# Rotary embedding of queries and keys: the swap of neighbouring partitions by VectorE or by transfers inside SBUF

## The chip, the cores and the metric

One core of a Trainium2 chip runs the whole kernel. The metric is the device time of one execution in microseconds; the kernel before takes 3115.08 us, the median of three runs (3113.67 to 3115.29).

## The reference

Two layers of a transformer decoder over 8 sequences of 256 tokens with 512 features. Layer 0 is causal attention in a window of 64 tokens with rotary embedding, cross attention to a context, and a mixture of 64 experts; layer 1 is a state-space mixer, cross attention and a feed-forward part with low-rank experts. What matters here is the rotary embedding:

```python
def _rotate_half(t):
    x1 = t[..., ::2]
    x2 = t[..., 1::2]
    return jnp.stack((-x2, x1), axis=-1).reshape(t.shape)
...
qkv = x @ w_qkv.T
...
q = q * cos + _rotate_half(q) * sin
k = k * cos + _rotate_half(k) * sin
scores = jnp.einsum('bhqd,bhkd->bhqk', q, k) * scale
```

Features 2j and 2j+1 are exchanged, one with its sign turned, multiplied by a sine and added to the cosine product.

## The kernel before

Everything that the change touches is in phase 1 (`phase1`), the first 750 us of the span: local attention and cross attention, one sequence after the other, i = 0 to 7. The engines run five programs of their own (`block.sync`, `block.gpsimd`, `block.scalar`, `block.tensor`, `block.vector`), each in the order written, and meet through semaphores that count up; `due(name, i, k)` is the count for the k-th event of sequence i.

Queries and keys are made with features on partitions and tokens in the free dimension: eight chunks of 128 features (four of queries, four of keys), 256 tokens each. The exchanged features are therefore neighbouring partitions. For each chunk c:

- TensorE (`queries_keys`, line 757) makes the product in bank 2 + c % 2, from weights and columns split in a high and a low part, twelve products per chunk (line 730). From chunk 2 on it waits until the copy of the chunk two before has left the bank (line 761).
- ScalarE (lines 661 to 664) copies the bank to `qk_raw`, a view of the first 2048 columns of the tile `arena`. In sequence 0 it also makes the high part of a piece of weights after each copy (`split_hi`).
- For each pair of chunks, n = 0 to 3, GpSimd (line 563) multiplies by the cosines into one of two buffers, `cosq` and `rec`. The third product waits for the first rotation to be added (line 562), the fourth for the second. Between the second and the third GpSimd computes the rstd of the previous sequence's output (line 567).
- VectorE (`rope`, line 955) exchanges neighbouring partitions with a shuffle into `sinq` (line 959), multiplies by the sines (line 960), and adds the cosine product into `qk` (line 962).

VectorE's order around this, for i of 1 and more, is: the end of the previous sequence's cross attention (`delta`, `centred`), rotation 0, the additions of that delta with their statistics (`add_delta`, two halves, lines 987 to 989), rotations 1 to 3, then the minima of the scores (line 1058). In sequence 0 two pieces of weights are split in their low part (`split_lo`, line 1013) after each rotation: the key weights after rotations 0 and 1, the value weights after 2 and 3; TensorE waits for these before chunks 4 to 7 and before the values.

TensorE makes the first half of the values after the eight chunks (`values(i, 0)`, from the buffer `w_slot`), then the scores of the first pair of heads, which need the third rotation (line 776); the fourth is needed from the fifth pair on. The second half of the values follows the second pair's scores.

SyncE's queue brings the value weights back from HBM in four pieces of 512 KB, one after each of the first four chunks (lines 501 to 503), for every sequence but the first. Later in a sequence it moves the values by half a tile into `v_mid` with two transfers inside SBUF, 64 partitions of 2 KB each (lines 460 and 461). ScalarE issues no transfer in this phase; in phase 2 it issues those that store expert outputs (`expert_out`).

`arena` is used in turn by `qk_raw`, by the transposed probabilities of local attention (first 1536 columns) and, whole, by the probabilities of cross attention. Once, at the start, the window mask is loaded into its columns 2048 to 2303 and copied to bf16.

Of the kernel before, what the change touches and what calls it, by code (L numbers as in the profile page):

```python
# [28 lines left out]
ALU = mybir.AluOpType  # L29
# [8 lines left out]
P = 128  # L38
NSEQ, S, D = 8, 256, 512
T = NSEQ * S  # L40
NT = S // P
KC = D // P
# [3 lines left out]
HD = D // HEADS  # L46
# [32 lines left out]
probs_ready probsT_psum probsT_ready pv_psum lrec_ready lrecT_psum lrec_copied xk_psum xk_ready xv_psum  # L79
xv_ready xq_psum xq_ready xs_psum clipped_ready xprobs_ready xpv_psum xrec_ready xrecT_psum xrec_copied  # L80
xattn_ready delta_psum delta_taken clip_bounds rs_ready shared_in init1 x_in ctx_in mask_in rows_out
wq_in w_hi w_lo vs_in slot_a slot_b colsT_lo hrT0_hi
""".split()
TURN_SEMS_2 = """
hThi_ready hTlo_ready sd_hi sd_lo router_psum negmax_router exp_router gate_psum tanh_ready
# [6 lines left out]
dtabs_ready dtexp_ready dtone_ready dtln_ready dA_ready tri_ready bc_psum decay_psum decay_ready  # L92
w_ready xrows_psum xrows_ready xdt_ready y_psum gated_ready sumsq_ready gated_norm
s_psum smin_ready sexp_ready sT_psum sT_act sT_dve ret_psum x_out_ready yk_used
routes_in cx_in cxT_in yk0_in0
""".split()


# [102 lines left out]
def due(name, i, k):  # L201

    return i * PER_SEQ[name] + k
# [130 lines left out]
def phase1(nc, sy, const, dr, held, nseq=NSEQ):  # L334
# [6 lines left out]
    with ExitStack() as ctx:  # L341
        def sb(name, shape, dt=F32):
            return ctx.enter_context(nc.sbuf_tensor(name, shape, dt))
# [3 lines left out]
        cosT, sinT = sb("cosT", [P, S]), sb("sinT", [P, S])  # L347
# [11 lines left out]
        oT = sb("oT", [P, KC, S])  # L359
        arena = sb("arena", [P, 4096])  # L360
        qk_raw = arena[:, 0:2 * KC * S].rearrange("p (c s) -> p c s", c=2 * KC)
        wmask = arena[:, 2048:2048 + S]
        qk = sb("qk", [P, 2 * KC, S])
        xkT = sb("xkT", [P, KC, S])
        cosq, sinq = sb("cosq", [P, 2, S]), sb("sinq", [P, 2, S])
        swap = [p ^ 1 for p in range(HD)]
        v, v_mid, xv = sb("v", [P, NT, D]), sb("v_mid", [P, D]), held["xv"]
        probs = sb("probs", [P, 3, 2, S])
        probsT = arena[:, 0:3 * 2 * S].rearrange("p (b k s) -> p b k s", b=3, k=2)
        smin, ssum = sb("lmin", [P, LPAIRS, 2, 2]), sb("lsums", [P, KC, NT, HPC])  # L370
        xprobs = arena[:].rearrange("p (b t k s) -> p b t k s", b=4, t=NT, k=2)
# [221 lines left out]
        def _(act):  # L593
            def split_hi(u, n):
                if u >= V:
                    act.wait_ge(sy[f"slot_{'ab'[u % 2]}"], stored(u - 2))
                    act.wait_ge(sy["qk_proj"], due("qk_proj", 0, KC * (u - 1)))
                if u == XQ:
                    act.wait_ge(sy["w1b_in"], n_late * 16)
                else:  # L600
                    act.wait_ge(sy["wq_in" if u == Q else "w1_in"], 16 if u == Q else n_early * 16)
                act.activation(w_slot[u % 2][:, n, 0, :], raw_piece(u, n), ACT.Copy).then_inc(sy["w_hi"], 1)

            def cols_copy(at):
                for j in range(NT):
                    act.wait_ge(sy["rowsT_psum"], at + j + 1)
                    act.activation(hT2[0][:, :, j * P:(j + 1) * P],  # L607
                                   turned_bank(at, j)[:, :].rearrange("p (c t) -> p c t", c=KC), ACT.Copy
                                   ).then_inc(sy["colsT_ready"], 1)

            def keys_copy(i, first, end):

                for c in range(first, end):
                    act.wait_ge(sy["xk_psum"], due("xk_psum", i, c + 1))
                    act.activation(xkT[:, c, :], key_bank(i, c)[:, 0:S], ACT.Identity, bias=bk[:, c:c + 1]
                                   ).then_inc(sy["xk_ready"], 1)

            def values_copy(i, j):
                act.wait_ge(sy["v_psum"], due("v_psum", i, j + 1))
                act.activation(v[:, j, :], bank(6 + j)[:, :], ACT.Copy).then_inc(sy["v_ready"], 1)  # L620

            def copy_recips(i, c):
                act.wait_ge(sy["lrecT_psum"], due("lrecT_psum", i, c + 1))
                if c >= 2:
                    act.wait_ge(sy["attn_ready"], due("attn_ready", i, c - 1))
                act.activation(rec[:, c % 2, :], bank(4 + c % 2)[:, S:2 * S], ACT.Copy
                               ).then_inc(sy["lrec_copied"], 1)
# [32 lines left out]
            for i in range(nseq):  # L660
                for c in range(2 * KC):
                    act.wait_ge(sy["qk_proj"], due("qk_proj", i, c + 1))
                    act.activation(qk_raw[:, c, :], bank(2 + c % 2)[:, 0:S], ACT.Copy,
                                   scale=-QK_SCALE if c < KC else 1.0).then_inc(sy["qk_raw_ready"], 1)
                    if i == 0:
                        split_hi(K if c < KC else V, c % KC)
                values_copy(i, 0)
                for n in range(LPAIRS):
                    c, r = n // 2, 2 * (n % 2)
                    act.wait_ge(sy["lmin_ready"], due("lmin_ready", i, n + 1))  # L670
                    if n >= 3:
                        act.wait_ge(sy["probsT_psum"], due("probsT_psum", i, n - 2))
                    for k in range(2):
                        scores = bank_pair(2 * (n % 2))[:, k, :]
                        act.activation(probs[:, n % 3, k, 0:P], scores[:, 0:P], ACT.Exp, bias=smin[:, n, k, 0:1],
                                       scale=-1.0, accum_out=ssum[:, c, 0, r + k:r + k + 1])
                        act.activation(probs[:, n % 3, k, P:S], scores[:, P:S], ACT.Exp,
                                       bias=smin[:, n, k, 1:2], scale=-1.0,
                                       accum_out=ssum[:, c, 1, r + k:r + k + 1]).then_inc(sy["probs_ready"], 1)
                    if n == 1:  # L680
                        values_copy(i, 1)
                    if i == 0 and 2 <= n < 2 + KC:
                        split_hi(XQ, n - 2)
                    if n in (5, 7):
                        copy_recips(i, (n - 5) // 2)
                copy_recips(i, 2)
                copy_recips(i, 3)
                if i == 0:
                    act.wait_ge(sy["w1b_in"], n_late * 16)
                    keys_copy(0, 0, KC)  # L690
                cols_copy(turned_attn(i))
                for c in range(KC):
                    act.wait_ge(sy["xq_psum"], due("xq_psum", i, c + 1))
                    act.activation(qk[:, c, :], bank(6 + c % 2)[:, 0:S], ACT.Identity, bias=bq[:, c:c + 1]
                                   ).then_inc(sy["xq_ready"], 1)
                for n in range(LPAIRS):
                    act.wait_ge(sy["clipped_ready"], due("clipped_ready", i, 2 * n + 2))
                    act.activation(xprobs[:, n % 4], xprobs[:, n % 4], ACT.Exp, scale=1.0 / ROOT_HD
                                   ).then_inc(sy["xprobs_ready"], 1)
                    if i < last and n in (0, LPAIRS - 1):  # L700
                        keys_copy(i + 1, n // (LPAIRS - 1), n // (LPAIRS - 1) + 1)
                    if i == last:
                        shared_opening(n)
                if i < last:
                    cols_copy(turned_in(i + 1))
                    keys_copy(i + 1, 2, 3)
                else:
                    shared_chunks_hi(2, 4)
                for half in range(2):
                    act.wait_ge(sy["xrecT_psum"], due("xrecT_psum", i, half + 1))  # L710
                    act.activation((cosq, sinq)[half][:].rearrange("p c s -> p (c s)"), bank(half)[:, :], ACT.Copy
                                   ).then_inc(sy["xrec_copied"], 1)
                if i < last:
                    keys_copy(i + 1, 3, KC)
                else:
                    shared_chunks_hi(4, len(MS_CHUNKS))
# [234 lines left out]
        def _(dve):  # L951
            def ln(ins):
                sy.link(dve, "dve_link", ins)

            def rope(i, n):
                dve.wait_ge(sy["qk_raw_ready"], due("qk_raw_ready", i, 2 * n + 2))
                if n:
                    dve.wait_ge(sy["rope_ready"], due("rope_ready", i, n))
                ln(dve.stream_shuffle(sinq[:], qk_raw[:, 2 * n:2 * n + 2, :], swap))
                ln(dve.tensor_tensor(sinq[:], sinq[:], sinT[:].unsqueeze(1).broadcast_to([P, 2, S]), ALU.mult))  # L960
                dve.wait_ge(sy["rope_cos_ready"], due("rope_cos_ready", i, n + 1))
                dve.tensor_tensor(qk[:, 2 * n:2 * n + 2, :], cosq2[n % 2][:], sinq[:], ALU.add
                                  ).then_inc(sy["rope_ready"], 1)
# [74 lines left out]
            for i in range(nseq):  # L1038
# [13 lines left out]
                for n in range(LPAIRS + 2):  # L1052
# [7 lines left out]
                    if n >= 2:  # L1060
                        m = n - 2
# [2441 lines left out]
```

## Time and profile before

| | us |
|---|---|
| median of three runs | 3115.08 |
| the profiled execution | 3110.33 |
| its span | 3108.5 |
| TensorE products busy | 2954.8 |
| VectorE busy | 2301.0 |
| ScalarE busy | 1579.0 |
| GpSimd busy | 808.7 |

Phase 1 ends near 750 us. A sequence takes about 90 us, and its rotation lies in the first 16 of them. Shares of busy time over the span say which engine is full on average; what one step is worth is read from the timeline around it and from the waits that end there. A row of a timeline has the start, the duration, the engine, the line, the operation, output and inputs, shapes and count of the merged instructions, and in brackets the idle time before them with what ended it. All times are microseconds from the start of the span unless marked as nanoseconds.

### The profile page before, as it was taken

Reading aid. Unit: us, or ns where it says so; the run is one execution under the profiler, and the core shown is the slowest. Engines: PE = TensorE matmul, PEld = TensorE weight load, DVE = VectorE, ACT = ScalarE, POOL = GpSimd, SP = SyncE. Lnnn points to the kernel's source line nnn. Section 1 sums busy time; section 2 is a strip of 40 time slices with the busy share of each in tenths; the row PEclk is TensorE's granted clock in tenths of the full one; section 3 lists DMA queues with packets and bytes.
Section 4 is the critical chain, followed back from the end, with each engine's and each line's share of the span. In section 5 each row is a group of like instructions: output and inputs, shape, how many; then the busy total and the mean of one; then the engine's idle time right before and its main releaser. Section 6 shows DMA issues by size and latency. Waiting matters only on the chain. (4 is left out here: it accounts for less than half of the span.)

```text
span 3108.5 us, 61772 instructions
## 1 busy us (share of the span) xinstructions
PE 2954.8 (95%) x23073; PEld 2384.2 (77%) x23073; DVE 2301.0 (74%) x4321; ACT 1579.0 (51%) x3643; POOL 808.7 (26%) x974
## 2 busy tenths in 40 slices
PE   7999999998999999999999969999999989999999
PEld 5666666665998888888888846767676678888888
DVE  5665666665876788888888668878786887777776
ACT  3323333333222555555555436666666765555554
POOL 1221122122664111111111073342412022222222
PEclk9999999999999999999999989999999999999999
DMA  7324333330312777777777642221210032222222
GB/s 281 116 93 188 126 140 112 126 113 29 119 56 65 235 244 248 236 249 237 250 244 243 229 142 65 69 73 56 69 42 18 33 125 75 76 79 80 76 69 72
DMA packets 146539, 403.96 MB, mean 130 GB/s; under 512 B 39488, under 2 KB 48192, under 8 KB 133520
## 3 DMA queue, kind: packets, MB, share of 16 engines
q1 hardware_dynamic: 107888, 325.36, 30.8%
q0 software_dynamic: 18976, 50.45, 5.7%
q10 hardware_dynamic: 19456, 25.18, 2.4%
q8 instruction: 143, 2.34, 0.3%
q14 instruction: 76, 0.62, 0.1%
HBM read 344.06 MB, written 54.76 MB: 128 GB/s over the span
## 5 line engine op out<-in xcount | busy, mean ns | idle before, releaser
L288 POOL DMA_INDIRECT hr<-normed_rows,idx x128 | 124.4, 972 | 629.2 <-PE psum L302 593.0
L3018 POOL TENSOR_TENSOR mixf<-act 128x256 f32<-128x256 f32 x128 | 143.2, 1119 | 458.6 <-DVE act L3284 458.6
L174 POOL TENSOR_SCALAR ve<-mv 128x1 f32<-128x1 f32 x112 | 35.9, 321 | 762.7 <-DVE mv L967 505.5
L328 PE MATMUL psum<-xT_hi,wgu_hi 128*128 128x192 f32 (+1 forms) x1536 | 228.4, 271 | 1.5 <-PEq L1127 0.9
L328 PE MATMUL psum<-xT_hi,wgu_lo 128*128 128x192 f32 (+1 forms) x1536 | 223.3, 268 | 0.0
L328 PE MATMUL psum<-xT_lo,wgu_hi 128*128 128x192 f32 (+1 forms) x1536 | 223.1, 268 | 0.0
L1744 ACT ACTIVATE eth<-psum 128x192 f32<-128x192 f32 (+1 forms) x192 | 63.2, 330 | 300.2 <-PE psum L328 293.5
L328 PEld LDWEIGHTS psum<-xT_hi,wgu_hi 128*128 128x128 f32 (+1 forms) x1536 | 190.3, 182 | 26.7 <-ACT wgu_hi L1728 21.5
L2312 ACT ACTIVATE scratch<-psum,smin 128x512 f32<-128x512 f32 x256 | 173.7, 687 | 62.3 <-DVE smin L2758 60.6
L328 PEld LDWEIGHTS psum<-xT_lo,wgu_hi 128*128 128x128 f32 (+1 forms) x1536 | 190.7, 183 | 0.0
L328 PEld LDWEIGHTS psum<-xT_hi,wgu_lo 128*128 128x128 f32 (+1 forms) x1536 | 190.5, 183 | 0.0
L3284 DVE TENSOR_TENSOR act<-act,maskT 128x512 f32<-128x512 f32 x128 | 88.1, 689 | 116.7 <-ACT act L3060 116.3
L2758 DVE TENSOR_REDUCE smin<-psum 128x2 f32<-128x1024 f32 x128 | 155.2, 1215 | 25.3 <-PE psum L2489 24.5
L2499 PEld LDWEIGHTS psum<-ident,scratch 128*128 128x128 f32 x1024 | 109.2, 141 | 59.0 <-issue 37.7
L2499 PE MATMUL psum<-ident,scratch 128*128 128x128 f32 x1024 | 145.3, 281 | 7.5 <-DVE scratch L2765 3.9
L1854 DVE SCALAR_TENSOR_TENSOR eact<-eth,psum 128x192 f32<-128x192 f32 (+1 forms) x192 | 67.5, 352 | 113.2 <-ACT eth L1744 110.8
L3294 DVE TENSOR_TENSOR ca_lo<-act,ca_hi 128x512 fp32r<-128x512 f32 x128 | 134.3, 1049 | 12.4
L730 PE MATMUL psum<-hT_hi,w_slot 128*128 128x256 f32 x768 | 110.8, 289 | 11.9 <-ACT hT_hi L607 5.9
L1267 POOL DMA_INDIRECT slot_token<-tok_i,slot_w x96 | 103.4, 1077 | 66.5 <-DVE slot_r L1592 41.6
L1098 DVE TENSOR_SCALAR arena<-psum,hi 128x512 f32<-128x512 f32 x128 | 87.5, 745 | 42.9 <-PE psum L836 42.9
L2126 POOL DMA_INDIRECT yk<-expert_out,slots x84 | 86.3, 1028 | 119.8 <-issue 48.4
L3073 ACT ACTIVATE ca_hi<-act 128x512 fp32r<-128x512 f32 x128 | 81.0, 633 | 66.5 <-DVE act L3284 66.5
(466 smaller groups left out, 8644.4 us busy)
## 6 DMA issues: line engine op xcount, KB each, us to landing
w_sg<-in_w_gu_dram SPq DMA_DIRECT2D x32, 1408.0 KB, 6.0
w_su<-in_w_gu_dram SPq DMA_DIRECT2D x32, 1408.0 KB, 5.9
w_slot<-w_split SPq DMA_DIRECT2D x21, 2048.0 KB, 8.9
w_raw<-in_w_dram SPq DMA_DIRECT2D x128, 256.0 KB, 2.6
w_sd<-in_w_d_dram SPq DMA_DIRECT2D x32, 512.0 KB, 8.7
wd<-in_w_d_dram SPq DMA_DIRECT2D x32, 512.0 KB, 8.6
expert_out<-so ACTq DMA_DIRECT2D x64, 256.0 KB, 5.3
w_slot<-w_split SPq DMA_DIRECT2D x28, 512.0 KB, 5.0
```

The source lines that it names most:

```text
L288: pool.indirect_dma_start(out=xg[0:w, t, :], out_offset=None, in_=rows, in_offset=bass.IndirectOffsetOnAxis(ap=idx[0:w, t:t + 1], axis=0)) ...
L328: ins = pe.matmul(bank(2 + m)[0:w, gu * CAP:(gu + 1) * CAP], wgu2[wp][:, gu, kc, m0:m0 + w], xT2[xp][:, kc, :], start=(i == 0 and kc == 0) ...
L730: ins = pe.matmul(out, lhs_of(lp, kc), rhs_of(rp, kc), start=(m == 0 and kc == 0), stop=(m == 2 and kc == KC - 1))
L1098: dve.tensor_scalar(xprobs[:, n % 4, kt], bank_pair(2 * (n % 2))[:, :, kt * S:(kt + 1) * S], hi[:, kt:kt + 1], -SCORE_CLIP * ROOT_HD, ALU. ...
L1267: pool.indirect_dma_start(out=dr["slot_token"], out_offset=bass.IndirectOffsetOnAxis(ap=slot_w[s % 2][:, j, k:k + 1], axis=0), in_=tok_i[s ...
L2126: pool.indirect_dma_start(out=gathered(s, NT * k + j), out_offset=None, in_=dr["expert_out"], in_offset=bass.IndirectOffsetOnAxis(ap=slots ...
L2312: act.activation(prob[:, q % 4, k, :], bank_pair(2 * (q % 2))[:, k, :], ACT.Exp, bias=smin[b][:, n, k:k + 1], scale=-1.0, accum_out=ssum[b ...
L2499: ins = pe.transpose(bank(4 + k)[:, mc * P:(mc + 1) * P], prob[:, q % 4, k, mc * P:(mc + 1) * P], ident)
L2758: dve.tensor_reduce(smin[(q // PAIRS) % 2][:, q % PAIRS, :], bank_pair(2 * (q % 2)), AX.X, ALU.min).then_inc(sy["smin_ready"], 1)
L3018: pool.tensor_tensor(mixf[:, g % LAG, :], act2[:, g % LAG, 0, :], act2[:, g % LAG, 1, :], ALU.add).then_inc(sy["f_mix"], 1)
L3284: dve.tensor_tensor(act2[:, g % LAG], act2[:, g % LAG], maskT[(g // FC) % 2][:, 2:4, :], ALU.mult).then_inc(sy["f_ca"], 1)
L3294: dve.tensor_tensor(ca2[1][:, g % LAG], act2[:, g % LAG], ca2[0][:, g % LAG].bitcast(F32), ALU.subtract).then_inc(sy["f_ca_lo"], 1)
```

## The change

ScalarE, after the copy of every second chunk, waits for this copy and issues two transfers inside SBUF: the odd partitions of two chunks of `qk_raw` go to the even partitions of a new view `qk_swap`, and the even to the odd. Each moves 64 partitions of 512 elements, 128 KB. `qk_swap` takes columns 2048 to 4095 of `arena`. VectorE waits for both transfers of a pair, and multiplies `qk_swap` by the sines straight into `sinq`; the shuffle and its list are gone. Each pair has a semaphore of its own (`swap0` to `swap3`). The window mask, which lay in the columns now taken, is loaded into a part of `probs`. Six more names in the third list of semaphores keep the three lists matched in length.

```diff
-wq_in w_hi w_lo vs_in slot_a slot_b colsT_lo hrT0_hi
+wq_in w_hi w_lo vs_in swap0 swap1 swap2 swap3 slot_a slot_b colsT_lo hrT0_hi
...
-routes_in cx_in cxT_in yk0_in0
+routes_in cx_in cxT_in yk0_in0 f_y f_mrow f_t2 f_t2m f_mix f_m
...
-        wmask = arena[:, 2048:2048 + S]
+        qk_swap = arena[:, 2 * KC * S:4 * KC * S].rearrange("p (c s) -> p c s", c=2 * KC)
...
-        swap = [p ^ 1 for p in range(HD)]
...
+        wmask = probs[:, 2, 0, :]
...
+            def swap_rows(i, n, m):
+                act.wait_ge(sy["qk_raw_ready"], due("qk_raw_ready", i, 2 * n + 2))
+                for odd in range(2):
+                    act.dma_start(qk_swap[odd:P:2, 2 * m:2 * m + 2, :], qk_raw[1 - odd:P:2, 2 * m:2 * m + 2, :]
+                                  ).then_inc(sy[f"swap{n}"], 16)
...
+                    if c % 2:
+                        swap_rows(i, c // 2, c // 2)
                     if i == 0:
                         split_hi(K if c < KC else V, c % KC)
...
-                ln(dve.stream_shuffle(sinq[:], qk_raw[:, 2 * n:2 * n + 2, :], swap))
-                ln(dve.tensor_tensor(sinq[:], sinq[:], sinT[:].unsqueeze(1).broadcast_to([P, 2, S]), ALU.mult))
+                dve.wait_ge(sy[f"swap{n}"], 32 * (i + 1))
+                ln(dve.tensor_tensor(sinq[:], qk_swap[:, 2 * n:2 * n + 2, :], sinT[:].unsqueeze(1).broadcast_to([P, 2, S]), ALU.mult))
```

## Rows read from the trace of the kernel before

**Rows 1.** The page, busy time of each engine and its share of the span.
```profile
PE 2954.8 (95%) x23073; PEld 2384.2 (77%) x23073; DVE 2301.0 (74%) x4321; ACT 1579.0 (51%) x3643; POOL 808.7 (26%) x974
```

**Rows 2.** Timeline of TensorE in the fourth sequence.
```profile
315.54 0.63 PE L730 MATMUL psum<-hT_lo,w_slot 128*128 128x256 f32 x4
316.06 2.10 PE L730 MATMUL psum<-w_slot,hT_hi 128*128 128x512 f32 x8
317.99 1.09 PE L730 MATMUL psum<-w_slot,hT_lo 128*128 128x512 f32 x4
320.25 0.38 PE L780 MATMUL psum<-wmask_b,ident_b 128*128 128x256 bf16 x2 [1.17 <-DVE qk L962]
...
322.48 3.67 PE L730 MATMUL psum<-w_slot,hT_hi 128*128 128x512 f32 x8
```

**Rows 3.** TensorE's waits, 100 to 740 us: for line 962, and for the value weights.
```profile
  PE psum L780: 6.0, 7
...
  DMA w_slot<-w_split: 1.8, 5
```

**Rows 4.** Timeline of VectorE in sequence 0.
```profile
20.21 0.77 DVE L959 STREAM_SHUFFLE sinq<-arena 128x512 f32<-128x512 f32 x1
...
22.72 2.38 DVE L1013 TENSOR_TENSOR w_slot<-w_su,w_slot 128x512 fp32r<-128x512 f32 x2
...
35.91 1.29 DVE L1013 TENSOR_TENSOR w_slot<-w_sd,w_slot 128x512 fp32r<-128x512 f32 x2
```

**Rows 5.** Timeline of TensorE in sequence 0, where the values start.
```profile
37.34 3.75 PE L730 MATMUL psum<-w_slot,hT_hi 128*128 128x512 f32 x8 [6.04 <-DVE w_slot L1013]
```

**Rows 6.** Line 959: shortest, median and longest in ns, first and last start.
```profile
L959 DVE STREAM_SHUFFLE sinq<-arena x32: 710/743/771, 20.2 to 681.0; 128x512 f32<-128x512 f32 x32
```

**Rows 7.** The tile v_mid: its transfers' issues in ns, and issue to landing.
```profile
L460 SPq DMA_DIRECT2D v_mid<-v x8: 467/467/550, 48.6 to 687.3; - x8
L461 SPq DMA_DIRECT2D v_mid<-v x8: 587/602/1906, 49.2 to 687.8; - x8
...
DMA to landing us min/median/max: 2.3/3.0/3.7
```

**Rows 8.** The page, DMA issues: count, KB each, median us to landing.
```profile
expert_out<-so ACTq DMA_DIRECT2D x64, 256.0 KB, 5.3
```

**Rows 9.** Timeline of ScalarE in the fourth sequence.
```profile
307.73 0.39 ACT L663 ACTIVATE arena<-psum 128x256 f32<-128x256 f32 x1 [1.03 <-PE psum L730]
309.14 0.39 ACT L663 ACTIVATE arena<-psum 128x256 f32<-128x256 f32 x1 [1.03 <-PE psum L730]
...
313.38 0.38 ACT L663 ACTIVATE arena<-psum 128x256 f32<-128x256 f32 x1 [1.02 <-PE psum L730]
```

**Rows 10.** Timeline of VectorE in the fourth sequence.
```profile
308.25 0.76 DVE L959 STREAM_SHUFFLE sinq<-arena 128x512 f32<-128x512 f32 x1
...
310.91 0.75 DVE L987 SCALAR_TENSOR_TENSOR so<-so,rstd 128x512 f32<-128x512 f32 x1
...
314.13 0.18 DVE L967 BATCH_NORM_AGGREGATE mv<-st 128x2 f32<-128x6 f32 x1
...
319.42 0.69 DVE L962 TENSOR_TENSOR qk<-cosq,sinq 128x512 f32<-128x512 f32 x1
```

**Rows 11.** Timeline of GpSimd in the fourth sequence.
```profile
315.23 1.61 POOL L563 TENSOR_TENSOR cosq<-arena,cosT 128x512 f32<-128x512 f32 x1
```

**Rows 12.** DMA, 304 to 318 us: busy tenths in 40 slices, SyncE's queue.
```profile
DMA  0000000005695979799899968797543200000000
...
q1 hardware_dynamic: 576, 2.10, 44.4%
```

**Rows 13.** DMA, 48 to 54 us, the v_mid pair alone: packets, MB, share of engines.
```profile
q1 hardware_dynamic: 160, 0.26, 19.3%
```

**Rows 14.** Timeline of ScalarE in sequence 0, the copy of chunk 5.
```profile
26.93 0.38 ACT L663 ACTIVATE arena<-psum 128x256 f32<-128x256 f32 x1 [0.78 <-PE psum L730]
```

**Rows 15.** Stretches of 2 us: busy time by engine, granted clock, DMA share, GB/s.
```profile
322.00:324.00 2.00, 2.00 (x16) 1.44 (x13) 2.00 (x5) 0.95 (x5) 0.00 (x0) 0.66 0.00 0
```

## The prediction

> **What bounds the kernel now.** I read four views in this order. First the busy shares: TensorE is busy in 95% of the span and VectorE in 74% [rows 1], so freed VectorE time is worth something only where TensorE waits for VectorE. Second, TensorE's timeline around the rotation of one sequence. I take the fourth; sequences 1 to 7 repeat it to a few tenths of a microsecond. The last key chunk ends at 315.54 + 0.63 = 316.2, the first half of the values runs from 316.06 to 319.08, then TensorE idles 1.17 us until the third rotation (the first pair of keys) is added, and scores start at 320.25 [rows 2]. Third, the sums of those waits from 100 to 740 us: 6.0 us in seven sequences for the rotation, and 1.8 us in five for the values' weights, a DMA load that lands at the moment it is needed [rows 3]. Fourth, the DMA view, because the change moves work onto those transfer engines. So the whole rotation now costs TensorE 6.0 us in sequences 1 to 7, and that is the most that a faster rotation can give there. Sequence 0 is different: VectorE is the bound, and TensorE waits 6.04 us for it before the values [rows 4, 5].
>
> **What is removed.** 32 shuffles of 743 ns [rows 6], 23.8 us of VectorE. Nearly all of it lies beside TensorE's work, which is why the bound above matters and this sum doesn't.
>
> **What is added.** Per sequence four pairs of transfers of 128 KB each (64 partitions of 2 KB), on ScalarE's queue, each behind the copy of the second chunk of its pair; VectorE waits for both of a pair. The nearest rows are the two v_mid transfers: same size, also inside SBUF, on SyncE's queue. One takes 467 or 602 ns to issue and lands 2.3 to 3.7 us after its issue, median 3.0 [rows 7]. The latency L from the end of the copy is then about 0.1 (wait for its own copy) + 0.47 (first issue) + landing of the second: 2.9 us with 2.3, 3.6 with 3.0, 4.3 with 3.7, and 5.9 with 5.3, which is what 256 KB take on ScalarE's queue beside weight loads [rows 8].
>
> **ScalarE's queue.** Behind the two issues stands the copy of the next chunk. It now starts after 1.03 us of idleness [rows 9], and TensorE wants its bank one chunk (1.41 us) after the result, while the copy takes 0.39: it may be late by some 0.8 us. Two issues of 0.47 + 0.60 and the wait make 1.2 us, so it is late by 0.2: nothing. If an issue takes the longest 1.9 us [rows 7], the pair takes 2.5 and TensorE loses 0.7 at each of the first three pairs. The wait for the own copy costs ScalarE 0.1 to 0.2, inside the same room.
>
> **The rotation in sequences 1 to 7.** In the fourth sequence the second copy ends at 308.12 [rows 9]. Before, the shuffle started at 308.25; after, VectorE stands until 308.12 + 3.6 = 311.7. Rotation 0 is then two operations of 0.69 (1.45 with gaps): 313.15. Behind it on VectorE stand the two delta additions with their statistics, 3.4 us (310.91 to 314.31) [rows 10]: 316.55. GpSimd waits for these statistics, computes rstd, and then starts the third cosine product, which ended 316.84, 2.53 after the statistics [rows 10, 11]: now 319.1. Rotation 1 ends at 318.1 to 318.8, the third at 319.8 to 320.2, against 320.11 before [rows 10]. With L of 2.9 or 4.3 this moves by 0.7 either way: the third rotation is between 0.8 us earlier and 0.8 later, in the middle 0. Four shuffles saved (3.0 us) pay for one exposed latency (3.6) and little else. The last rotation is needed only by the fifth pair of heads and by the minimum behind it on VectorE, and has us of room.
>
> **The values' load.** It has no room. Its four pieces (2.10 MB) take 44.4% of 14 us, 6.2 us of all 16 engines; they move from 307.3 to 315.5, with 1.9 us of those 8.2 unused [rows 12]. A pair of v_mid transfers took 19.3% of 6.0 us, 1.16 us of all engines [rows 13]; by bytes alone, at the load's rate, it would be 0.78. I take 1.0. The pairs of copies ending at 308.1, 310.9 and 313.8 [rows 9] bring their data ahead of the load's end, since the load ends later by what they take: 3.0 us of work. If the unused 1.9 us take up all they can, the load ends 1.1 later; if nothing, at 1.16 each, 3.5 later. I take 1.8, between 1.1 and 3.0, nearer to the first because the engines are free at different moments. The Trainium skill speaks against the change here: its page "DMA: Bandwidth & Descriptors", section "Issuing engines are not separate DMA queues", says that transfers from different issuing engines run on the same 16 DMA engines and interleave. If it holds, the second queue protects nothing; if it does not, the case below with free transfers stands.
> TensorE starts the values with the load. Five sequences already wait; for the other two I give 0.3 us each of room. The wait for the rotation behind the values absorbs 6.0 us in all. Sum: 7 x 1.8 - 0.6 - 6.0 = +6.0 us. With 1.1: +1.1. With 3.5: +17.9. With no delay of the load the rotation decides: 7 x -0.8 to +0.8, -5.6 to +5.6.
>
> **Sequence 0.** VectorE splits the weights between rotations, TensorE waits for the splits, and the initial loads fill the DMA engines. I take L = 4.0, between 2.9 and 5.9. The first shuffle starts at 20.21, just after the copy at 20.07 [rows 4]. After: rotation 0 from 24.1 to 25.5; two splits (2.38) to 27.9; rotation 1 to 29.35; two splits to 31.7. The copy of chunk 5 ended 27.31, 4.6 after its splits began at 22.72 [rows 4, 14]; now 25.5 + 4.6 = 30.1, its swap lands 34.1, rotation 2 and two splits end 37.9. The copy of chunk 7: 29.35 + 4.6 = 33.95, landed 37.95; rotation 3 to 39.4, the last splits (1.29) to 40.7, against 37.20: +3.5 us. The same with L = 2.9: 38.5, +1.3; with 5.9: 44.5, +7.3. TensorE starts the values right behind [rows 5].
>
> **Sum.** +6.0 + 3.5 = +9.5 us on the profiled execution (3110.3, span 3108.5): 3119.8. The median of the runs is 4.8 above it, 3115.1, and by it I forecast 3124.6, rounded to 3124.5. The other semaphores and the mask's new place cost nothing: a program of the same loads, with the mask read once at the start.
>
> **Rivals.**
> Free transfers, faster: the swap pairs fit into unused DMA time, land after 2.9 us, and the third rotation comes 0.8 earlier: -5.6 + 1.3 = -4.3 us, 3110.8. For it: v_mid landed in 2.3 us when alone. Against: the load's engines are 75% busy, and five of seven sequences already wait for it. To be faster by over 0.2% it would have to recover all 6.0 us and gain in sequence 0 too.
> Free transfers, no gain: the load is hardly delayed, the rotation stays where it is, only sequence 0 pays: +1 to +4, 3116 to 3119.
> The wait turns into a slow clock: in the fourth sequence TensorE's granted clock was 0.66 of full in 322 to 324, a mixture of the 2.4 GHz and the 1.2 GHz level [rows 15], after the idle 1.17 us, and eight products took 3.67 us and not 2.10 [rows 2]. If waits of 2 us in front of the values bring that in all seven sequences, 7 x 1.57 = 11 us come on top: 3135.5. Against: only one of seven idles of about 1 us was followed by it.
> ScalarE's issues block: 3 x 0.7 x 7 = 15 us on top of the rest at worst, about 3139. It decides from an issue pair above 1.9 us; the median of the same row is 0.6.
>
> **How the numbers follow.** Forecast 0.48, own range 3118 to 3133. Free, no gain 0.25. Free and faster 0.09. Slow clock 0.12. Blocked issues 0.06. A kernel of this spread tells 0.2% (6.2 us) from no change: below 3108.9 is faster, above 3121.3 slower. Faster: 0.04. Slower: three quarters of the forecast and both last rivals, 0.54. Same: 0.42. Range 3111 to 3140, from the bounds -4.3 and +25 (17.9 + 7.3).
>
> **What would show it.** Right: TensorE's wait for w_slot grows from 1.8 us to 10 or more and its wait for the rotation shrinks towards zero; VectorE waits about 3.6 us at the first rotation; the values of sequence 0 start near 40.8. Wrong: the wait for w_slot stays under 4 us (transfers free), or the wait for the rotation grows (L above 4.3), or TensorE waits for the raw copies (issues block), or the granted clock drops in more sequences.

## The result: 60 us slower, and the profile after

The changed kernel takes 3175.51 us (median of four runs, 3170.54 to 3180.78) against 3115.18 for the kernel before in the same comparison: ratio 1.0194, 95% interval 1.0178 to 1.0210. The forecast was 3124.5 with a range to 3140. Its direction was right, its size was a sixth of what came.

The page of the changed kernel, against [rows 1]: VectorE's busy time fell by 35 us, TensorE's rose by 23 with the same number of products. Of the 35 us, 24 are the shuffles and 7 the sine products, of which the kernel before ran some beside GpSimd's cosine products.

```profile
span 3172.3 us, 61772 instructions
...
PE 2978.0 (94%) x23073; PEld 2398.4 (76%) x23073; DVE 2266.2 (71%) x4257; ACT 1580.7 (50%) x3643; POOL 811.4 (26%) x974
```

All of the difference arises in phase 1. The first gate product of the routed experts (line 328, whose row also has the first and the last start) is a marker behind it; here the kernel before, then the changed one:

```profile
L328 PE MATMUL psum<-xT_hi,wgu_hi x1536: 247/273/528, 998.4 to 1776.6; 128*128 128x192 f32 x128, 128*96 128x192 f32 x64
```
```profile
L328 PE MATMUL psum<-xT_hi,wgu_hi x1536: 247/273/358, 1064.1 to 1838.6; 128*128 128x192 f32 x128, 128*96 128x192 f32 x64
```

It is 65.7 us later, and the span 63.8 us longer. I use this marker below, since what follows it differs by some microseconds from one trace to the next (2107.4 to 2114.0 us from the marker to the end, over all kernels here). It is read from one profiled execution of each kernel, so its own scatter is not shown. Lines from 615 on have moved down in the changed kernel: the sine product is 968, the rotation's addition 970, the wait for it ends at 788, the projections' products are 738.

Waits of the changed kernel, 17 to 790 us (us in total, times, longest), against [rows 3, 5]:

```profile
DVE sinq L968 <- DMA arena<-arena: 72.7, 10, 11.5
...
PE psum L788 <- DVE qk L970: 31.2, 7, 5.2
...
PE psum L738 <- DVE w_slot L1021: 20.1, 2, 13.0
...
PE psum L738 <- DMA w_slot<-w_split: 7.5, 7, 1.6
```

VectorE now stands 72.7 us before sine products, 48.3 at the first rotation of sequences 1 to 7 and 24.4 in sequence 0. That is three times the 23.8 us of shuffles it was spared. TensorE's wait for the rotation in sequences 1 to 7 grew from 6.0 to 31.2 us, its wait for the value weights from 1.8 to 7.5.

The fourth sequence of the changed kernel, first ScalarE and its queue, then VectorE, GpSimd and TensorE, against [rows 2, 9, 10, 11]:

```profile
335.96 0.39 ACT L669 ACTIVATE arena<-psum 128x256 f32<-128x256 f32 x1 [1.01 <-PE psum L738]
336.38 1.12 ACTq L621 DMA_DIRECT2D arena<-arena  x2
```
```profile
342.95 0.69 DVE L968 TENSOR_TENSOR sinq<-arena,sinT 128x512 f32<-128x512 f32 x1 [6.67 <-DMA arena<-arena]
...
347.39 0.18 DVE L975 BATCH_NORM_AGGREGATE mv<-st 128x2 f32<-128x6 f32 x1
...
350.92 1.67 DVE L970 TENSOR_TENSOR qk<-cosq,sinq 128x512 f32<-128x512 f32 x1 [1.22 <-POOL cosq L563]
```
```profile
348.35 0.99 POOL L175 TENSOR_TENSOR rstd<-ve,minus_half 128x1 f32<-128x1 f32 x1
349.31 1.50 POOL L563 TENSOR_TENSOR cosq<-arena,cosT 128x512 f32<-128x512 f32 x1
350.78 1.25 POOL L563 TENSOR_TENSOR rec<-arena,cosT 128x512 f32<-128x512 f32 x1
```
```profile
345.24 2.10 PE L738 MATMUL psum<-w_slot,hT_hi 128*128 128x512 f32 x8 [0.67 <-DMA w_slot<-w_split]
347.18 1.09 PE L738 MATMUL psum<-w_slot,hT_lo 128*128 128x512 f32 x4
352.73 0.58 PE L788 MATMUL psum<-wmask_b,ident_b 128*128 128x256 bf16 x2 [4.47 <-DVE qk L970]
...
356.51 3.78 PE L738 MATMUL psum<-w_slot,hT_hi 128*128 128x512 f32 x8
...
361.80 0.65 PE L788 MATMUL psum<-wmask_b,ident_b 128*128 128x256 bf16 x2
```

The copy ends at 336.35, the exchanged rows can be read at 342.95: a latency of 6.6 us. Everything behind it on VectorE moves, then GpSimd's third product, and the addition of the third rotation ends at 352.6. TensorE, done with the values at 348.3, idles 4.47 us. And then it is slow: eight products of 512 columns take 3.78 us, not 2.10, and from the first to the third pair's scores pass 361.80 - 352.73 = 9.1 us, where the kernel before took 5.1 in six of its seven sequences (6.7 in this one, the only one whose clock fell there [rows 2, 15]). The granted clock says why (stretches of 2 us: busy time per engine, granted clock, DMA share, GB/s): after the wait it is at its lower level, 1.2 GHz.

```profile
350.00:352.00 2.00, 0.00 (x0) 0.00 (x0) 1.08 (x1) 0.00 (x0) 2.00 (x3) 1.00 0.00 0
352.00:354.00 2.00, 1.27 (x10) 0.67 (x10) 1.88 (x3) 0.00 (x0) 1.83 (x4) 0.52 0.00 0
354.00:356.00 2.00, 2.00 (x20) 1.04 (x22) 0.78 (x2) 0.53 (x3) 0.14 (x1) 0.50 0.00 0
```

Sequence 0 of the changed kernel, VectorE and then TensorE, against [rows 4, 5]: the first and the third rotation wait 11.4 and 11.5 us, the second 1.5, and the values start at 50.33 and not at 37.34.

```profile
26.79 0.69 DVE L968 TENSOR_TENSOR sinq<-arena,sinT 128x512 f32<-128x512 f32 x1 [11.40 <-DMA arena<-arena]
...
45.03 0.69 DVE L968 TENSOR_TENSOR sinq<-arena,sinT 128x512 f32<-128x512 f32 x1 [11.50 <-DMA arena<-arena]
```
```profile
50.33 3.75 PE L738 MATMUL psum<-w_slot,hT_hi 128*128 128x512 f32 x8 [12.96 <-DVE w_slot L1021]
```

The account of the 65.7 us at the marker: sequence 0, 13.0; in sequences 1 to 7 the wait for the rotation, 31.2 - 6.0 = 25.2; the wait for the value weights, 7.5 - 1.8 = 5.7; the clock, 21.2 (first to third scores take 8.38 us in the mean of the seven, 5.35 before: 7 x 3.03). Together 65.1. This adds up waits, not causes. The rotation is now ready 3.8 to 5.2 us behind the values, so a value load that came on time would only lengthen the wait for the rotation: its 5.7 us are not a cost of their own.

### The profile page after: what moved, and what is told of

Read it like the earlier page. It is cut to its first block and busy times, and to the rows that moved or that the text cites. A ratio compares the mean times of both kernels' runs of the same rounds, so it can differ in the third digit from the quotient of the medians.

```text
span 3172.3 us, 61772 instructions
## 1 busy us (share of the span) xinstructions
PE 2978.0 (94%) x23073; PEld 2398.4 (76%) x23073; DVE 2266.2 (71%) x4257; ACT 1580.7 (50%) x3643; POOL 811.4 (26%) x974
## 5 line engine op out<-in xcount | busy, mean ns | idle before, releaser
L738 PEld LDWEIGHTS psum<-hT_hi,w_slot 128*128 128x128 f32 x768 | 99.3, 193 | 24.4 <-issue 10.6
```

The source lines that it names most:

```text
L738: ins = pe.matmul(out, lhs_of(lp, kc), rhs_of(rp, kc), start=(m == 0 and kc == 0), stop=(m == 2 and kc == KC - 1))
```

## The experiments

All times are medians beside the kernel before on the same chip (3111 to 3114 there), and the ratio is to that. "Marker" is the start of the first gate product: 998.4 before, 1064.1 changed. The expectations count from 3115 us before; where a time lies near one of their bounds, I also give the ratio times 3115, "on their scale". Edits are to the changed kernel unless said otherwise.

**Is it the transfers' traffic, or waiting for them?** Shuffles kept and used, transfers issued beside them:

```diff
+        swap = [p ^ 1 for p in range(HD)]
...
-                dve.wait_ge(sy[f"swap{n}"], 32 * (i + 1))
-                ln(dve.tensor_tensor(sinq[:], qk_swap[:, 2 * n:2 * n + 2, :], sinT[:].unsqueeze(1).broadcast_to([P, 2, S]), ALU.mult))
+                ln(dve.stream_shuffle(sinq[:], qk_raw[:, 2 * n:2 * n + 2, :], swap))
+                ln(dve.tensor_tensor(sinq[:], sinq[:], sinT[:].unsqueeze(1).broadcast_to([P, 2, S]), ALU.mult))
...
+                    if n == 2:
+                        for m in range(KC):
+                            dve.wait_ge(sy[f"swap{m}"], 32 * (i + 1))
```

> The shuffles are kept and used; the transfers are issued as in the changed kernel, but nobody waits for them before the third minimum of the scores. Theory of exposed latency (the 60 us are VectorE's wait for the transfers and what follows from it): 3116 to 3122, the value weights' load being some 0.8 us later per sequence, mostly inside TensorE's wait for the rotation. Rival of contention (the transfers' traffic or their issue on ScalarE slows the rest): 3160 or more.

Measured: 3111.3, ratio 1.0008 (0.9994 to 1.0022), 3117.5 on their scale and so inside the theory's 3116 to 3122, marker 997.6. The 64 transfers with all their traffic and their issue on ScalarE's queue cost nothing that can be told from zero. The waits, 17 to 820 us, show how: the load of the value weights is late, but the time comes out of the wait behind it, which falls from 6.0 to 0.4 us, as the prediction had it.

```profile
PE psum L739 <- DMA w_slot<-w_split: 8.3, 7, 1.6
...
PE psum L789 <- DVE qk L971: 0.4, 2, 0.2
```

One pair of issues took 2.2 us in this run, and TensorE waited 0.34 us for the copy behind it: the rival of blocked issues exists, and is small.

**What was there to gain?** No exchange, no transfers:

```diff
-                dve.wait_ge(sy[f"swap{n}"], 32 * (i + 1))
-                ln(dve.tensor_tensor(sinq[:], qk_swap[:, 2 * n:2 * n + 2, :], sinT[:].unsqueeze(1).broadcast_to([P, 2, S]), ALU.mult))
+                ln(dve.tensor_tensor(sinq[:], qk_raw[:, 2 * n:2 * n + 2, :], sinT[:].unsqueeze(1).broadcast_to([P, 2, S]), ALU.mult))
...
-                    if c % 2:
-                        swap_rows(i, c // 2, c // 2)
```

> The changed kernel with no exchange at all: no transfers, no wait, the sine product reads the unexchanged copies (left out: the exchange of neighbouring features). It gives the most that taking the shuffle away can be worth. By the theory that TensorE waited 6.0 us for the rotation in sequences 1 to 7 and that sequence 0 holds four shuffles (3.0 us) on VectorE's chain: 3115 - 6 - 3 = 3106. The rival, that VectorE's busy time is the bound in phase 1, gives 3115 - 24 = 3091.

Measured: 3101.0, ratio 0.9969 (0.9957 to 0.9982), 9.6 us by the ratio; marker 987.4, 11.0 earlier. So the ceiling read from the waits (9 us) holds, and the 23.8 us of shuffles are not worth their sum even when they cost nothing to replace.

**Where does the latency come from?** Once without the load beside it, once with another layout of the same bytes:

```diff
-                        load_unit(V, n, n + 1)
+                        sp.dma_start(w_slot[0][0:16, n:n + 1].bitcast(F32), dr["w_split"][V, 0:16, n:n + 1]
+                                     ).then_inc(sy["slot_a"], 16)
```

> The changed kernel with the value weights' load of sequences 1 to 7 cut to 16 of 128 partitions (left out: the other value weights, so the values are those of stale weights). Theory that the latency of 6.6 us is made by the load on the same transfer engines: it falls to some 3 to 3.7 us, TensorE's wait before the scores falls below 1.5 us, the clock stays full, and only sequence 0 stays slow: 3124 to 3130. Rival, that the transfer itself takes that long (every second partition, ScalarE's queue): latency stays above 6, time above 3165.

```diff
-                    act.dma_start(qk_swap[odd:P:2, 2 * m:2 * m + 2, :], qk_raw[1 - odd:P:2, 2 * m:2 * m + 2, :]
+                    act.dma_start(qk_swap[odd * HALF:(odd + 1) * HALF, 2 * m:2 * m + 2, :], qk_raw[(1 - odd) * HALF:(2 - odd) * HALF, 2 * m:2 * m + 2, :]
```

> The changed kernel with the same bytes moved between the two halves of 64 neighbouring partitions, as the v_mid transfers do, and not between every second one (left out: the right exchange). Theory of the load: nothing changes, 3170 to 3180. Rival of the layout (a stride of two partitions is slow): latency falls to 3 to 4 us, time to 3135 or less.

Measured with the small load: 3156.0, ratio 1.0143 (1.0118 to 1.0168), marker 1041.9; the expectation of 3124 to 3130 failed. With the halves: 3175.3, ratio 1.0205 (1.0180 to 1.0230), as the load theory has it. Issue to landing of the transfers, in the changed kernel, with the small load, and with the halves:

```profile
DMA to landing us min/median/max: 1.9/4.4/9.5
```
```profile
DMA to landing us min/median/max: 1.9/2.1/9.3
```
```profile
DMA to landing us min/median/max: 2.5/5.3/10.1
```

The load makes the latency of sequences 1 to 7: with the small load the median falls from 4.4 to 2.1 us, and from the end of the copy to the first sine product pass 3.0 us in five sequences, 3.6 and 4.2 in the others, where the changed kernel has 6.6 to 7.2. Every second partition is no slow layout; with the halves, which I had taken for a model in the v_mid transfers, that time is the same for the first pair (6.6 to 7.1), the median over all pairs is longer, and TensorE's wait for the value weights doubled (15.9 us). But the kernel with the small load was still 43.5 us slow at the marker, 13.8 of it in sequence 0, which the edit leaves alone. By this run, contention with the load carries 22 of the 65.7 us. Its fifth sequence, VectorE, GpSimd, then TensorE:

```profile
432.15 1.76 DVE L969 TENSOR_TENSOR sinq<-arena,sinT 128x512 f32<-128x512 f32 x1 [3.08 <-DMA arena<-arena]
...
437.65 0.18 DVE L976 BATCH_NORM_AGGREGATE mv<-st 128x2 f32<-128x6 f32 x1
...
441.19 1.66 DVE L971 TENSOR_TENSOR qk<-cosq,sinq 128x512 f32<-128x512 f32 x1 [1.23 <-POOL cosq L564]
```
```profile
432.06 1.29 POOL L564 TENSOR_TENSOR rec<-arena,cosT 128x512 f32<-128x512 f32 x1 [1.30 <-ACT arena L670]
...
441.05 1.26 POOL L564 TENSOR_TENSOR rec<-arena,cosT 128x512 f32<-128x512 f32 x1
```
```profile
443.00 0.38 PE L789 MATMUL psum<-wmask_b,ident_b 128*128 128x256 bf16 x2 [2.97 <-DVE qk L971]
```

The copy ended at 429.15: latency 3.0 us, better than the 3.6 of the prediction, and TensorE still waits 2.97 us. Three things made the difference that the prediction had too short: a sine product of 1.76 us beside GpSimd's second cosine product, where it had 0.69; a third cosine product that ends 3.3 us behind the statistics, where it had 2.53, and for which VectorE waits 1.23 us; and an addition of 1.66 us beside GpSimd's fourth, where it had 0.69. The clock fell again in all seven sequences: first to third scores take 8.1 us in the mean, which is 19 us of the 43.5.

**GpSimd's part.** The rstd taken out of its way:

```diff
-                    if n == 1 and i >= 1:
+                    if n == KC - 1 and i >= 1:
                         rstd_pool(pool, sy, norm_out(i - 1), mv, ve, rstd, const["minus_half"])
```

> The changed kernel with GpSimd's rstd of the previous sequence's output behind the fourth cosine product and not ahead of the third. Theory (the third rotation is late not only by the transfers, but because GpSimd gets to the third product after the delayed statistics and VectorE then adds beside GpSimd's next product): the wait for the third product (1.2 us) goes, TensorE's wait falls from 4.5 to 2 or 2.5 us, clock loss shrinks: 3150 to 3160. Rival (only the landing of the transfers counts): 3172 or more.

Measured: 3165.9, ratio 1.0169 (1.0150 to 1.0187), 3167.6 on their scale, marker 1051.8, 12.3 us earlier than the changed kernel. TensorE's wait for the rotation fell from 31.2 to 23.0 us, so 1.2 us of 4.5 per sequence were the rstd's; it was expected to fall to 2 or 2.5 per sequence and fell to 3.3, and the time lies between the two theories. The addition beside GpSimd's fourth product stayed at 1.63 us, and no run takes that product away from it: this part of the price is read from the traces alone.

**The order on VectorE.** The additions of the delta into the wait:

```diff
+                if i >= 1:
+                    for j in range(NT):
+                        add_delta(i - 1, j)
                 for n in range(KC):
                     rope(i, n)
...
-                    if i >= 1 and n == 0:
-                        for j in range(NT):
-                            add_delta(i - 1, j)
```

> The changed kernel with the additions of the previous delta and their statistics put ahead of rotation 0 on VectorE, so that 3.4 us of work lie inside the wait for the transfers. Theory (in-order VectorE carries the latency through these additions and GpSimd's rstd and third cosine product to the third rotation): rotation 0 starts as late as before, but the third rotation ends about when the first values do, TensorE's wait before the scores falls from 4.5 to under 0.5 us and the clock stays full: 3175 - 45 = 3130. Rival (the late transfers of the third pair themselves are what TensorE waits for): the wait stays above 3 us, 3165 or more.

Measured: 3145.3, ratio 1.0107 (1.0085 to 1.0128), marker 1036.4: 27.7 us back by the marker, where 45 were expected; the time lies between the theory's 3130 and the rival's 3165. The wait before the scores fell to 1.2 to 2.0 us, not under 0.5, and the clock still fell for part of the stretch (8.1 us from first to third scores in three sequences, 6.6 to 6.7 in four). The second pair of transfers now also makes VectorE wait, 0.73 us, and the third addition again runs beside GpSimd:

```profile
335.97 0.69 DVE L968 TENSOR_TENSOR sinq<-arena,sinT 128x512 f32<-128x512 f32 x1 [3.50 <-DMA arena<-arena]
...
338.12 1.24 DVE L968 TENSOR_TENSOR sinq<-arena,sinT 128x512 f32<-128x512 f32 x1 [0.73 <-DMA arena<-arena]
...
340.91 1.64 DVE L970 TENSOR_TENSOR qk<-cosq,sinq 128x512 f32<-128x512 f32 x1
```

**The clock.** The same waiting time, with work in it:

```diff
                     values(i, 0)
+                    products(bank(4)[:, :], lambda p, kc: hT2[p][:, kc, 0:P],
+                             lambda p, kc: w_slot[0][:, kc, p, :], PRODUCTS)
```

> The changed kernel with twelve more products on TensorE (a repetition of the first values into a free bank, 3.1 us, their result unused) between the values and the wait for the rotation. Theory of the clock (4.5 us of idleness halve the granted clock for the next 9 us): the clock stays full, 2.4 to 3.9 us per sequence come back: 3175 - 17 to 27 = 3148 to 3158. Rival (the clock falls for the whole load of the phase, not for the idleness): 3175 or more.

```diff
                     values(i, 0)
+                    for m in range(18):
+                        pe.matmul(bank(4)[:, :], hT2[0][:, m % KC, 0:P], w_slot[0][:, m % KC, 0, :], start=True, stop=True)
```

> The changed kernel with eighteen products of 512 columns on TensorE (about 4 us, result unused) between the first values and its wait for the rotation. Theory of the clock: the first scores start as late as in the changed kernel but at full clock in all seven sequences, so first to third scores take 5.1 us in place of 7.8 to 9.1: 3175 - 22 = 3153. Rival (the twelve products that came before kept the clock in three of seven sequences by chance): no more than those, 3163 or more.

Measured with twelve products: 3164.9, ratio 1.0169 (1.0147 to 1.0191), marker 1054.3; idle before the scores was 1.1 to 2.2 us, and the clock stayed full in three of seven sequences; the 3148 to 3158 expected were missed. With eighteen: 3158.8, ratio 1.0150 (1.0134 to 1.0165), marker 1045.8. On their scale this is 3161.7, with an interval that holds the rival's 3163 and not the theory's 3153, so the time alone would not decide; the trace does. Its fourth sequence:

```profile
343.18 4.36 PE L775 MATMUL psum<-w_slot,hT_hi 128*128 128x512 f32 x18
347.78 0.38 PE L790 MATMUL psum<-wmask_b,ident_b 128*128 128x256 bf16 x2 [0.24 <-DVE qk L972]
...
350.00 2.13 PE L738 MATMUL psum<-w_slot,hT_hi 128*128 128x512 f32 x8
```

TensorE has more to do and is sooner done. The rotation came as late as before (scores start 7.35 us after the values, 7.49 in the changed kernel, in the mean of seven), and first to third scores took 5.1 us in six of seven, 6.7 in the other: 5.36 in the mean against 8.38. That is 21 us for the clock alone; the marker moved by 18.3, since the wait for the value weights was 3.2 us longer. The idleness, and not the load of the phase, brings the clock down.

**Sequence 0, and both repairs together.**

```diff
-                    if c % 2:
+                    if c % 2 and i >= 1:
                         swap_rows(i, c // 2, c // 2)
...
-                dve.wait_ge(sy[f"swap{n}"], 32 * (i + 1))
+                if i >= 1:
+                    dve.wait_ge(sy[f"swap{n}"], 32 * i)
+                if i == 0:
+                    ln(dve.stream_shuffle(sinq[:], qk_raw[:, 2 * n:2 * n + 2, :], swap))
+                src = qk_swap[:, 2 * n:2 * n + 2, :] if i >= 1 else sinq[:]
...
```

> The changed kernel with the shuffle and no transfers in sequence 0, transfers from sequence 1 on. Theory: the 13.0 us by which the values of sequence 0 start later come back, the rest stays: 3162. Rival (part of it is absorbed later by the loads of the start): 3168 or more.

> Both: the shuffle in sequence 0, and the delta's additions ahead of rotation 0 from sequence 1 on. Theory: 3175 - 13 - 45 = 3117, no difference from the kernel before, because TensorE then waits for the value weights' load instead (1.1 us per sequence). If the load is delayed less than that, 3112. Rival (a cost that neither edit touches): 3125 or more.

Measured: 3166.1 for the first, ratio 1.0173 (1.0152 to 1.0195), marker 1053.0, 11.1 us earlier than the changed kernel. On their scale it is 3168.9, with an interval of 7 us to either side, which does not tell the theory from the rival; the trace shows where the time went. The values of sequence 0 started at 37.77 and not at 50.33, 12.6 us, and 1.5 of these were lost again by the marker. For both together 3127.8, ratio 1.0063 (1.0040 to 1.0086), marker 1014.8. That is beyond the rival's 3125 and not the theory's 3117: 16 us at the marker are left. No new cost is needed for them: TensorE still waits 9.0 us for the rotation and 8.9 for the value weights (7.8 together before), which is 10 us, and the clock fell in three sequences, which is 6 (first to third scores, against the kernel before).

**A transfer that nobody waits for.** Only the fourth pair, whose transfers start when the load is done; the other pairs keep the shuffle (VectorE's side is not shown):

```diff
-                    if c % 2:
+                    if c == 2 * KC - 1 and i >= 1:
...
```

> Transfers for the fourth pair alone and from sequence 1 on, shuffles for all others: 14 transfers in place of 64. Its transfers start when the value weights have landed and it is needed only by the fifth pair of heads. Theory (what costs is a latency that is waited for, not a transfer): latency about 3 us, hidden in the rotation before, ratio to the kernel before 0.999 to 1.001. Rival (any transfer from ScalarE's queue costs by its issue): 1.003 or more.

Measured: 3111.9, ratio 1.0000 (0.9991 to 1.0010), marker 996.4. Issue to landing:

```profile
DMA to landing us min/median/max: 1.9/2.0/2.8
```

Its latency is hidden, so it costs nothing, and since the fourth rotation gates nothing, it brings nothing.

**What the profile pointed to instead.** The kernel before, with shuffles, the delta's additions moved:

```diff
-                    if i >= 1 and n == 0:
+                    if i >= 1 and n == 2:
                         for j in range(NT):
                             add_delta(i - 1, j)
...
-                    if n == 1 and i >= 1:
+                    if n == KC - 1 and i >= 1:
                         rstd_pool(pool, sy, norm_out(i - 1), mv, ve, rstd, const["minus_half"])
```

> The kernel before, with shuffles and no transfers; only the additions of the previous delta move behind the third rotation on VectorE, and GpSimd's rstd for them behind the fourth cosine product. Theory (TensorE waits 6.0 us in sequences 1 to 7 because 3.4 us of additions stand ahead of the third rotation): that wait goes to zero, the load's wait grows a little, ratio to the kernel before 0.998. Rival (the additions, now later, delay the minima of the scores): 1.000 or more.

Measured: 3104.7, ratio 0.9973 (0.9963 to 0.9983), marker 989.3: faster than the kernel before by 0.27%, a small gain that is clear of the interval. TensorE no longer waits for the rotation at all, and the scores follow the values directly:

```profile
315.68 1.09 PE L730 MATMUL psum<-w_slot,hT_lo 128*128 128x512 f32 x4
316.61 0.39 PE L780 MATMUL psum<-wmask_b,ident_b 128*128 128x256 bf16 x2
```

## Why the prediction was wrong, step by step

**The bound.** Right. Waits of 6.0 us and a chain in sequence 0 gave a ceiling of 9 us; without any exchange 9.6 were measured.

**The latency L.** This is the step that failed first, and by the small load it carries 22 of the 65.7 us. "3.6 with 3.0" was taken for sequences 1 to 7, with 4.3 as the upper bound, from v_mid, whose transfers run when the value weights have landed (the fourth sequence's load ends at 315.5 [rows 12], its values are made after that). It was 6.6 to 7.2 us in all seven. The row of 5.3 us [rows 8], from the very queue and beside weight loads, was known and was kept for sequence 0 alone, although [rows 12] show the same engines 76% busy (6.2 us of the load's 8.2) in sequences 1 to 7. It gives 5.9 and would have been nearer, though still 0.7 to 1.3 us short. Where a transfer joins a busy stretch, the row from a busy stretch is the near one. While both queues had work, the engines gave them this (DMA, 338 to 342 us of the changed kernel: packets, MB, share):

```profile
q1 hardware_dynamic: 249, 0.90, 76.1%
q10 hardware_dynamic: 156, 0.26, 18.0%
```

ScalarE's queue moved 0.26 MB in these 4 us, as much as one pair has; alone, a pair took 1.16 us of the engines [rows 13]. What divides the engines between the queues so unequally stays open.

**"Four shuffles saved pay for one exposed latency and little else."** Wrong in itself, and the larger failure. My sum for sequences 1 to 7 was -5.6 us with L = 2.9 and a load that is not delayed; with the small load, and L at 3.0 in five of them, they are some 30 us slower (43.5 less 13.8). Step by step: with L = 6.6 my own steps give 342.95 + 1.45 + 3.4 = 347.8 for the statistics, 350.3 for the third product and 351 for the rotation, a wait of 2.7 us; it was 4.47. With L = 3.0 they give 319.2 for the rotation in the fourth sequence of the kernel before, 0.1 behind the values; with the small load the wait was 2.97. The missing 1.8 us of the changed kernel are GpSimd's rstd and third product, 3.2 us behind the statistics and not 2.53 (0.7), and VectorE's addition of 1.67 us beside GpSimd's fourth product (1.0). With the small load the sine product of 1.76 us comes on top (1.1).

The prediction had carried over durations of operations whose neighbours on the other engine it had just moved, and for the addition it took the short one, 0.69. The trace of the kernel before had the long ones already, twenty-one in sequences 1 to 7, among them these of VectorE in the fourth (GpSimd's products ended there at 309.72 and 316.84):

```profile
309.04 1.23 DVE L960 TENSOR_TENSOR sinq<-sinq,sinT 128x512 f32<-128x512 f32 x1
...
315.74 1.66 DVE L962 TENSOR_TENSOR qk<-rec,sinq 128x512 f32<-128x512 f32 x1
```

In all twenty-one, and in the seven of the changed kernel, VectorE's operation ends 0.54 to 0.56 us after GpSimd's product, wherever in that product it began. So its price can be worked out: what is left of GpSimd's product, and 0.55 us.

**The values' load.** The mechanism was right, the size too high: it became later by 0.8 to 0.9 us per sequence (TensorE's waits 7.5 or 8.3 against 1.8) and not 1.8. Of the 6.5 us by which this wait grew beside the kept shuffles, none is seen at the marker: the wait behind it took them in. So this term, the main one of the forecast in sequences 1 to 7, costs nothing, and that the direction came out right there is luck. The Trainium skill says that transfers from different issuing engines interleave on the same 16 DMA engines ("DMA: Bandwidth & Descriptors", "Issuing engines are not separate DMA queues"). The trace agrees: between 338 and 342 us both queues moved data. But it hit the other way round. The small transfers suffered from the load, by 3.6 us (L of 6.6 against 3.0 with the small load), more than the load from them, by 0.9.

**Sequence 0.** The chain was right, L was not: 7.3 us for the first pair, 8.5 for the second and 10.2 for the third (copy at 34.83, read at 45.03), not 4.0 or at most 5.9; TensorE, idle for 7.11 us, did the next chunks at the lower clock, so that the copy of chunk 5 ended 6.7 us after the splits began and not 4.6. While the third pair waited, from 34 to 46 us, SyncE's queue had 78% of the engines; that its loads make the latency here too was not tested. +13.0 us against +3.5, bounds 1.3 to 7.3.

**The slow clock.** It stood among the rivals with 0.12 and 11 us. It came in all seven sequences and cost 21 us, twice the 11, since I had counted eight slow products (1.57 us) and the whole stretch to the third scores loses 3.03. I had made it depend on waits of 2 us before the values; with L right, the wait before the scores would have been seen to be 2.7 us or more, and the rival would have been part of the forecast. Two of the prediction's own signs of being wrong came: the wait for the rotation grew, and the clock dropped in more sequences.

**ScalarE's queue.** Right: two issues took 1.12 us, the next copy was late by 0.2, and TensorE waited for no copy, the longest pair being 1.8 us. Beside the kept shuffles it waited 0.3 us once, after a pair of 2.2.

## What to carry to other kernels

Before an in-order engine is relieved of an operation by a transfer, ask what it will do in the meantime: here 0.74 us of work became 6.6 us of standing, with 3.4 us of independent work queued behind the wait. Where the transfer moves work of one engine beside work of another, take the durations again as they are beside that neighbour. Take the latency from a row in which the transfer engines are as busy as they will be there, not from the transfer of the same size. And when the profile shows TensorE waiting 0.9 us for a step, look first at what stands ahead of that step in the queue: moving 3.4 us of other work behind it, and GpSimd's rstd with it, gave 7.5 us here (3112.2 to 3104.7), most of what removing every shuffle gives.

## What the runs showed of the hardware that I had not expected

- Two transfers of 128 KB inside SBUF, every second partition: issue to landing 2.0 us in the median with free engines, 4.4 beside a load from HBM that takes 76% of them, up to 9.5 in sequence 0, where the engines are over 90% busy for 8 us on end. The same bytes between two halves of 64 neighbouring partitions: 5.3 us in the median beside the load, and TensorE's wait for the load was twice as long (15.9 us against 7.5).
- VectorE's product and addition of 128x512 with two inputs in SBUF take 0.69 us alone. Begun beside such a product on GpSimd they end 0.54 to 0.56 us after it, and so take 1.05 to 1.76 us in the traces of the kernel before, the changed kernel and the small load.
- TensorE at 1.2 GHz after idle stretches of 3.8 to 5.2 us costs two thirds of the idleness once more (21 us behind 31). After 1.1 to 2.2 us it fell in four of seven sequences with twelve products, in three of six with both repairs, and for a part of the stretch in all seven with the additions first; filling the wait with eighteen unused products kept it up in six of seven.
